# Transformer block with experts on Trainium2: low float16 parts of q, k and the attention output by VectorE from PSUM, in place of a ScalarE copy and a GpSimd subtraction

## Chip, cores and metric

One core of a Trainium2 chip (trn2). The metric is the device time of one execution in microseconds; lower is better.

## The reference, cut to what matters

Eight batches of 512 tokens of width 256 pass an adaptive layer norm, attention with 16 heads of 16, a second layer norm and a mixture of 2 shared and 16 routed experts (4 of 16 chosen for a token), all in float32:

```python
h = _layernorm(x, axis=-1) * (1 + ca) + sa
q, k, v = (split_heads(h @ w + b) for w, b in ((wq, bq), (wk, bk), (wv, bv)))
attn = softmax(einsum('bhqd,bhkd->bhqk', q, k) / 4)
o = einsum('bhqk,bhkd->bhqd', attn, v)            # heads merged
x = x + ga * (o @ wo + bo)
h = _layernorm(x, axis=-1) * (1 + cb) + sb
shared = gelu(h @ shared_up.T) @ shared_down.T     # 2 experts
routed = (gelu(h @ routed_up.T) * gate) @ routed_down.T  # 16 experts, gate from the top 4 probabilities
x = x + gb * (shared + routed)
```

## The kernel before, in words

**Split operands.** TensorE multiplies float16. A float32 value v is held as hi = float16(v) and lo = float16(v - hi), and a product is the sum of three: hi·hi, lo·hi and hi·lo (`split_product`). This concerns the layer norm's rows transposed (h1T, h2T: h and z), the attention output transposed (onT: z), q and k (qk), the experts' activations (act) and the weights.

**How a low part is made.** For h1T, h2T, onT and qk the result stands in a PSUM bank. ScalarE (`split_out`, line 668) copies it to float16 (line 671, `qk_hi`, `z_hi`, `h_hi`), then a second time as float32 into one of the two slots of `f_ring` in SBUF (line 673); this copy gives the bank back to TensorE (semaphore `taken[kind]`). GpSimd, which has no access to the bank in this kernel, then subtracts (`lo_part`, line 592): lo = f_ring - hi. The low part's own semaphore lets its users go on (the output projection for onT, the store to HBM for qk), and frees the slot of `f_ring`.

**Order.** All five engines walk one list, `PLAN`, written by a planner from tables of places, and each does the part of an item that is its own, in this order. A "slot" of the list is one group of 16 score products for the maxima (kind max: TensorE makes scores 128x512, VectorE takes their row maxima, line 907), one group of 16 for the softmax of an earlier group (kind exp: TensorE, then ScalarE, line 715), the value products (pv, line 1026; o_raw at line 898 is the copy of their result), and experts of an earlier batch: up (line 950, then gelu, line 750), gated (VectorE times the gate, line 894), act_hi (ScalarE, line 692), act_lo (GpSimd, line 651), down (line 1118). The maxima of four groups are transposed (maxT) and put by ScalarE or VectorE into the operand `q_aug`, from which the scores of kind exp then come with the maximum subtracted. Before item group 6 (about 180 us) there are no experts' products to fill the gaps; from there on the work repeats from batch to batch.

**Banks.** VectorE's items have three PSUM banks (`vector_bank`), ScalarE's three (`scalar_bank`), the experts' sums two (`down_bank`, lent to the others until the experts begin). Each item takes the bank that was used longest ago, and TensorE waits until that user's result has been taken (`wait_bank`). The order and the bank of every item are fixed when the program is built.

**The units that the change touches.** qk: 2 units for b = 0 (its first scores come from a shorter way, kind first) and 4 for each other batch, 30 in all, here called first to fourth unit of a batch; onT: 2 for each batch, 16 in all. Those of q and k of batch b stand in the slots that handle the scores of batch b - 1.

**GpSimd early on.** The item "fill" (lines 597 to 601) sets constants in the second pair of score operands and in `v_aug`; then come the steps of the layer norm's reciprocal deviation (line 584 to 586), for which VectorE's `rows` of the next batch (line 767) wait.

## Time and profile before

| | us |
|---|---|
| median of 3 runs | 887.67 |
| lowest, highest | 886.67, 888.42 |
| the profiled execution | 887.85 |
| its span, first to last instruction | 886.1 |
| TensorE busy (matmul) | 834.1, 94% |
| weight loads, beside them | 450.5, 51% |
| VectorE | 607.6, 69% |
| ScalarE | 681.8, 77% |
| GpSimd | 395.8, 45% |

In the profile PE is TensorE, PEld its weight loads, DVE VectorE, ACT ScalarE, POOL GpSimd. "L907" is line 907 of the kernel. A name such as `neg_max<-vector_bank` says what an instruction writes and reads, "128x512 f32" its shape and type, "x484" how many there are. In the timeline, neighbours of one form are merged to one row with their number; a bracket tells how long the engine was idle before, and what ended it. "Granted clock" is TensorE's clock as a share of 2.4 GHz; its mean over the span is 0.976, and in the stretches from 180 to 785 us it is 1.00.

### The profile page before, as it was taken

The page shows a single profiled execution, that of the slowest core. Times are in us where ns is not written, and L with a number is a line of the kernel's source. Part 1 is how long each engine was busy: PE and PEld are TensorE (multiplying, and loading weights), DVE is VectorE, ACT ScalarE, POOL GpSimd, SP SyncE. Part 2 cuts the span into 40 slices and gives each one's busy share as a digit, 9 for nine tenths or more (in the row PEclk, how much of TensorE's full clock was granted, in tenths as well). Part 3 has the DMA queues.
Part 4 walks back from the last instruction along what each step waited for, and adds up shares of the span by engine and source line. Part 5 has one row for each costly group of instructions (what it writes and reads, how often), then busy time and mean ns, then how long its engine had stood idle before and what let it go on. Part 6 is the DMA issues. An engine that isn't in the chain of part 4 may idle for free.

```text
span 886.1 us, 19423 instructions
## 1 busy us (share of the span) xinstructions
PE 834.1 (94%) x7652; PEld 450.5 (51%) x7652; DVE 607.6 (69%) x1211; ACT 681.8 (77%) x1158; POOL 395.8 (45%) x349
## 2 busy tenths in 40 slices
PE   5858788999999999999999999999999999998998
PEld 4322133355545575566545655566555554555555
DVE  4675677777688866977588776976687668632452
ACT  5468878878997789878988889878987788855452
POOL 4365215224744255335633464426623263346472
PEclk9987889899999999999999999999999999999999
DMA  7024400344025221424025402431314300330140
GB/s 259 13 75 131 137 13 14 97 127 138 13 61 175 90 61 52 148 62 138 25 68 169 138 2 73 154 100 25 105 48 149 119 2 1 133 120 1 61 163 26
DMA packets 47290, 77.18 MB, mean 87 GB/s; under 512 B 6392, under 2 KB 41432, under 8 KB 43104
## 3 DMA queue, kind: packets, MB, share of 16 engines
q1 hardware_dynamic: 47200, 75.94, 27.1%
q8 instruction: 61, 1.00, 0.5%
q14 instruction: 29, 0.24, 0.1%
HBM read 63.47 MB, written 12.34 MB: 86 GB/s over the span
## 4 chain that ended last, share of the span: by engine, by line
PE 74%; ACT 9%; DVE 8%; POOL 4%; issue 3%; DMA 0%; ACTq 0%; DVEq 0%
PE scalar_bank L950 21%; PE down_bank L1118 18%; PE vector_bank L1026 9%; PE scalar_bank L1009 6%; PE vector_bank L1009 6%; PE vector_bank L950 5%; DVE neg_max L907 3%; PE scalar_bank L1038 3%; ACT q_aug L701 2%; ACT probs L715 2%; PE vector_bank L1050 2%; ACT rows L684 1%; DVE gelu L894 1%; ACT f_ring L673 1%; PE scalar_bank L1062 1%
## 5 line engine op out<-in xcount | busy, mean ns | idle before, releaser
L907 DVE TENSOR_REDUCE neg_max<-vector_bank 128x1 f16<-128x512 f32 x484 | 306.7, 686 | 84.9 <-PE vector_bank L1009 75.6
L715 ACT ACTIVATE probs<-scalar_bank 128x512 f32<-128x512 f32 x486 | 262.3, 605 | 41.9 <-PE scalar_bank L1009 39.2
L651 POOL TENSOR_TENSOR act_lo<-gelu,act_hi 128x512 f16<-128x512 f32 x144 | 172.7, 1217 | 164.9 <-ACT act_hi L692 146.8
L1118 PE MATMUL down_bank<-down_hi,act_hi 64*128 64x256 f16 x1120 | 174.8, 271 | 0.4 <-PE down_bank L1118 0.2
L1118 PE MATMUL down_bank<-down_lo,act_hi 64*128 64x256 f16 x1120 | 173.7, 269 | 0.0
L1118 PE MATMUL down_bank<-down_hi,act_lo 64*128 64x256 f16 x1120 | 173.7, 269 | 0.0
L1009 PE MATMUL vector_bank<-k_aug,q_aug 64*128 64x512 f16 x484 | 132.9, 393 | 13.9 <-ACT q_aug L701 7.4
L894 DVE TENSOR_TENSOR gelu<-gelu,gates 128x512 f32<-128x512 f32 x128 | 110.3, 882 | 47.7 <-ACT gelu L750 47.4
L1009 PE MATMUL scalar_bank<-q_aug,k_aug 64*128 64x512 f16 x486 | 126.3, 389 | 3.9 <-ACT probs L715 1.7
L750 ACT ACTIVATE gelu<-scalar_bank 128x512 f32<-128x512 f32 x144 | 85.0, 596 | 57.6 <-PE scalar_bank L950 39.0
L1026 PE MATMUL vector_bank<-probs,v_aug 128*32 128x512 f32 x992 | 117.0, 601 | 0.0
L950 PE MATMUL scalar_bank<-z_hi,up_hi 128*128 128x512 f16 x288 | 109.9, 382 | 0.0
L950 PE MATMUL scalar_bank<-z_lo,up_hi 128*128 128x512 f16 x288 | 109.5, 380 | 0.0
L950 PE MATMUL scalar_bank<-z_hi,up_lo 128*128 128x512 f16 x288 | 109.4, 380 | 0.0
L692 ACT ACTIVATE act_hi<-gelu 128x512 f16<-128x512 f32 x128 | 76.8, 624 | 25.3 <-DVE gelu L894 19.0
L1118 PEld LDWEIGHTS down_bank<-down_hi,act_hi 64*128 64x128 f16 x1120 | 70.3, 94 | 47.8 <-issue 36.3
L1118 PEld LDWEIGHTS down_bank<-down_lo,act_hi 64*128 64x128 f16 x1120 | 74.8, 94 | 8.2
L1118 PEld LDWEIGHTS down_bank<-down_hi,act_lo 64*128 64x128 f16 x1120 | 74.7, 94 | 4.9
L1009 PEld LDWEIGHTS vector_bank<-k_aug,q_aug 64*128 64x128 f16 x484 | 37.1, 95 | 57.0 <-DVE neg_max L907 21.8
L592 POOL TENSOR_TENSOR z_lo<-f_ring,z_hi 128x512 f16<-128x512 f32 x32 | 36.6, 1155 | 56.5 <-ACT f_ring L673 56.5
L1009 PEld LDWEIGHTS scalar_bank<-q_aug,k_aug 64*128 64x128 f16 x486 | 37.3, 94 | 45.4 <-ACT probs L715 21.7
L1026 PEld LDWEIGHTS vector_bank<-probs,v_aug 128*32 128x32 f32 x992 | 27.5, 109 | 62.2 <-issue 56.6
(200 smaller groups left out, 1255.2 us busy)
## 6 DMA issues: line engine op xcount, KB each, us to landing
gates<-gates_by_expert SPq DMA_DIRECT2D x32, 1024.0 KB, 5.2
q_aug<-q_parts SPq DMA_DIRECT2D x90, 64.0 KB, 2.7
k_aug<-k_parts SPq DMA_DIRECT2D x90, 64.0 KB, 3.1
x_pre<-in_x SPq DMA_DIRECT2D x8, 512.0 KB, 4.6
x_post<-in_x SPq DMA_DIRECT2D x8, 512.0 KB, 6.5
out<-x_post SPq DMA_DIRECT2D x16, 256.0 KB, 3.6
gates<-in_w_up SPq DMA_DIRECT2D x4, 576.0 KB, 11.2
gates<-in_w_down SPq DMA_DIRECT2D x4, 576.0 KB, 4.5
```

The source lines that it names most:

```text
L592: pool.tensor_tensor(lo, f_ring[:, F_RING[kind, n, b][0], :], hi, ALU.subtract).then_inc(s_lo, 1)
L651: pool.tensor_tensor(act[1][:, c, :], gelu[:, n % NGELU, :], act[0][:, c, :], ALU.subtract).then_inc(s_elo, 1)
L692: scalar.activation(act[0][:, act_slot(b, n), :], gelu[:, n % NGELU, :], ACT.Copy).then_inc(s_ehi, 1)
L715: scalar.activation(probs[:, n % U, :], src[:], ACT.Exp, scale=SCALE).then_inc(taken[kind], 1)
L750: scalar.activation(gelu[:, n % NGELU, :], src[:], ACT.Gelu).then_inc(taken[kind], 1)
L894: dve.tensor_tensor(g, g, gates[:, (n - NSH) % 8, :], ALU.mult).then_inc(s_gated, 1)
L907: dve.tensor_reduce(neg_max[:, (u // 2) % TT, at:at + 1], src[:], AX.X, ALU.max, negate=True).then_inc(done, 1)
L950: ins = pe.matmul(dst, a, b, start=n == 0, stop=n == len(terms) - 1)
L1009: pe.matmul(dst[:], st[at:at + 64, pair, t * P:(t + 1) * P], mo[at:at + 64, pair, :], start=True, stop=True).then_inc(sig, 1)
L1026: ins = pe.matmul(o, v_aug[b % 2][:, kc, h * VW:h * VW + 32], probs[:, u, :], start=kc == 0, stop=kc == TT - 1)
L1038: ins = pe.transpose(dst[:, t * P:(t + 1) * P], a[:, t, n * P:(n + 1) * P], ident[:])
L1118: ins = pe.matmul(o, act[a][at:at + 64, act_slot(b, c), tok:tok + P], wd[w][at:at + 64, c, :], start=n == 0 and k == 0, stop=c == NEX - 1 ...
```

## The change

The units qk and onT no longer use `f_ring`. ScalarE makes the high part alone and signals it (`qk_hi_made`, `attention_hi_made`). VectorE, at the unit's own place in the list, waits for that signal and makes the low part in one instruction from the PSUM bank: for qk (bank + bias) - hi, for onT bank - hi. The semaphore of the low part is now also the one that gives the bank back to TensorE. GpSimd does nothing for these units. h1T, h2T and first are as before, and have the two slots of `f_ring` to themselves. TensorE's order is unchanged.

```diff
-F_KINDS = ("first", "onT", "h1T", "qk", "h2T")
+F_KINDS = ("first", "h1T", "h2T")
...
+        hi_made = {"qk": sem("qk_hi_made"), "onT": sem("attention_hi_made")}
+        taken["qk"], taken["onT"] = s_qklo, s_onlo
...
-                elif kind == "qk":
-                    lo_part(kind, n, b, qk[0][:, n % 2, :], qk[1][:, n % 2, :], s_qklo)
...
-                elif kind == "onT":
-                    lo_part(kind, n, b, z[0][:, n, :], z[1][:, n, :], s_onlo)
...
-                    split_out(item, src[:], qk[0][:, n % 2, :], ACT.Identity, bias=bqk[:, n % 2 * 2 + n // 2:n % 2 * 2 + n // 2 + 1])
+                    scalar.activation(qk[0][:, n % 2, :], src[:], ACT.Identity,
+                                      bias=bqk[:, n % 2 * 2 + n // 2:n % 2 * 2 + n // 2 + 1]).then_inc(hi_made["qk"], 1)
...
-                    split_out(item, src[:], z[0][:, n, :], ACT.Copy)
+                    scalar.activation(z[0][:, n, :], src[:], ACT.Copy).then_inc(hi_made["onT"], 1)
...
+                elif kind == "qk":
+                    wait(dve, hi_made["qk"], 4, b, n + 1 - SKIPPED["qk"])
+                    dve.scalar_tensor_tensor(qk[1][:, n % 2, :], bank(item)[:], bqk[:, n % 2 * 2 + n // 2:n % 2 * 2 + n // 2 + 1],
+                                             qk[0][:, n % 2, :], ALU.add, ALU.subtract).then_inc(s_qklo, 1)
+                elif kind == "onT":
+                    wait(dve, hi_made["onT"], 2, b, n + 1)
+                    z = z2[b % 2]
+                    dve.tensor_tensor(z[1][:, n, :], bank(item)[:], z[0][:, n, :], ALU.subtract).then_inc(s_onlo, 1)
```

VectorE around the second and third q and k unit of b = 3 (the timeline's 240 to 253 us; line 907 of before is line 914 of the change, 898 is 897, 939 is 946). Before:

```order
L894 TENSOR_TENSOR gelu<-gelu,gates 128x512 [waits taken_up] x3
L907 TENSOR_REDUCE neg_max<-vector_bank 128x1 [waits made_max] x2
L898 COPY o_raw<-vector_bank 128x512 [waits made_pv,made_oT]
L907 TENSOR_REDUCE neg_max<-vector_bank 128x1 [waits made_max] x12
L939 COPY logits<-vector_bank 128x64 [waits made_logit]
```

and with the change:

```order
L893 TENSOR_TENSOR gelu<-gelu,gates 128x512 [waits taken_up]
L900 SCALAR_TENSOR_TENSOR qk_lo<-scalar_bank,bqk,qk_hi 128x512 [waits qk_hi_made]
L893 TENSOR_TENSOR gelu<-gelu,gates 128x512 [waits taken_up] x2
L914 TENSOR_REDUCE neg_max<-vector_bank 128x1 [waits made_max] x2
L897 COPY o_raw<-vector_bank 128x512 [waits made_pv,made_oT]
L914 TENSOR_REDUCE neg_max<-vector_bank 128x1 [waits made_max] x2
L900 SCALAR_TENSOR_TENSOR qk_lo<-scalar_bank,bqk,qk_hi 128x512 [waits qk_hi_made]
L914 TENSOR_REDUCE neg_max<-vector_bank 128x1 [waits made_max] x4
L900 SCALAR_TENSOR_TENSOR qk_lo<-scalar_bank,bqk,qk_hi 128x512 [waits qk_hi_made]
L914 TENSOR_REDUCE neg_max<-vector_bank 128x1 [waits made_max] x6
L946 COPY logits<-vector_bank 128x64 [waits made_logit]
```

Three low parts now stand in the row, one between gate products and two between maxima.

VectorE around the fourth unit of b = 3 (260 to 267 us), where the router's last steps (865 to 873 of the change, 866 to 874 of before) stand. Before:

```order
L907 TENSOR_REDUCE neg_max<-vector_bank 128x1 [waits made_max] x2
L894 TENSOR_TENSOR gelu<-gelu,gates 128x512 [waits taken_up]
L866 TENSOR_REDUCE top<-e 128x4 [waits router_exp]
L894 TENSOR_TENSOR gelu<-gelu,gates 128x512 [waits taken_up]
L869 RECIPROCAL top<-top 128x4 [waits router_steps]
L871 TENSOR_TENSOR chosen<-chosen,e 128x64 [waits router_steps]
L874 TENSOR_TENSOR chosen<-chosen,top 128x64 [waits router_steps]
L898 COPY o_raw<-vector_bank 128x512 [waits made_pv,made_oT]
```

and with the change:

```order
L914 TENSOR_REDUCE neg_max<-vector_bank 128x1 [waits made_max] x2
L900 SCALAR_TENSOR_TENSOR qk_lo<-scalar_bank,bqk,qk_hi 128x512 [waits qk_hi_made]
L893 TENSOR_TENSOR gelu<-gelu,gates 128x512 [waits taken_up]
L865 TENSOR_REDUCE top<-e 128x4 [waits router_exp]
L893 TENSOR_TENSOR gelu<-gelu,gates 128x512 [waits taken_up]
L868 RECIPROCAL top<-top 128x4 [waits router_steps]
L870 TENSOR_TENSOR chosen<-chosen,e 128x64 [waits router_steps]
L873 TENSOR_TENSOR chosen<-chosen,top 128x64 [waits router_steps]
L897 COPY o_raw<-vector_bank 128x512 [waits made_pv,made_oT]
```

The low part comes ahead of both gate products and of the router's steps.

GpSimd around "fill" (43 to 55 us). Before:

```order
L629 TENSOR_TENSOR q_aug<-f_ring,act_hi 128x512 [waits taken_first]
L592 TENSOR_TENSOR qk_lo<-f_ring,qk_hi 128x512 [waits taken_qk]
L598 MEMSET q_aug 128x2048
L599 MEMSET k_aug 128x2048
L601 MEMSET v_aug 128x1152 x2
L584 TENSOR_SCALAR rstd<-mean_var 128x4 [waits ln1_steps]
```

and with the change:

```order
L631 TENSOR_TENSOR q_aug<-f_ring,act_hi 128x512 [waits taken_first]
L600 MEMSET q_aug 128x2048
L601 MEMSET k_aug 128x2048
L603 MEMSET v_aug 128x1152 x2
L586 TENSOR_SCALAR rstd<-mean_var 128x4 [waits ln1_steps]
```

The fills follow the operand of kind first directly.

## Rows read from the trace of the kernel before

**Rows 1.** the page's busy times; one stage: busy us by engine, clock, DMA
```profile
PE 834.1 (94%) x7652; PEld 450.5 (51%) x7652; DVE 607.6 (69%) x1211; ACT 681.8 (77%) x1158; POOL 395.8 (45%) x349
221.00:319.00 98.00, 97.73 (x959) 55.76 (x959) 75.50 (x151) 83.87 (x143) 45.22 (x40) 1.00 0.30 90
```

**Rows 2.** groups of instructions: busy us, mean ns of one, idle before them
```profile
L673 ACT ACTIVATE f_ring<-scalar_bank,bqk 128x512 f32<-128x512 f32 x28 | 19.3, 689 | 0.0
L592 POOL TENSOR_TENSOR qk_lo<-f_ring,qk_hi 128x512 f16<-128x512 f32 x30 | 35.5, 1184 | 42.4 <-ACT f_ring L673 42.4
L926 DVE TENSOR_TENSOR rows<-vector_bank,ga_all 128x512 f32<-128x512 f32 x15 | 10.4, 692 | 25.4 <-PE vector_bank L950 25.4
```

**Rows 3.** timeline, third unit, b = 3: start us, us, instruction, [idle before]
```profile
248.88 0.68 ACT L671 ACTIVATE qk_hi<-scalar_bank,bqk 128x512 f16<-128x512 f32 x1
249.16 3.08 DVE L907 TENSOR_REDUCE neg_max<-vector_bank 128x1 f16<-128x512 f32 x5 [0.91 <-PE vector_bank L1009]
249.83 0.47 PE L1009 MATMUL vector_bank<-k_aug,q_aug 64*128 64x512 f16 x2
```

**Rows 4.** timeline, attention output of b = 1
```profile
221.08 0.60 ACT L671 ACTIVATE z_hi<-scalar_bank 128x512 f16<-128x512 f32 x1
221.58 0.59 ACT L673 ACTIVATE f_ring<-scalar_bank 128x512 f32<-128x512 f32 x1
222.49 2.49 DVE L907 TENSOR_REDUCE neg_max<-vector_bank 128x1 f16<-128x512 f32 x4 [0.69 <-PE vector_bank L1009]
223.17 0.47 PE L1009 MATMUL vector_bank<-k_aug,q_aug 64*128 64x512 f16 x2
```

**Rows 5.** timeline, fourth unit of b = 3
```profile
262.19 0.69 ACT L671 ACTIVATE qk_hi<-scalar_bank,bqk 128x512 f16<-128x512 f32 x1
261.99 1.19 DVE L894 TENSOR_TENSOR gelu<-gelu,gates 128x512 f32<-128x512 f32 x1
263.93 1.09 DVE L871 TENSOR_TENSOR chosen<-chosen,e 128x64 f32<-128x64 f32 x1
265.05 1.08 DVE L874 TENSOR_TENSOR chosen<-chosen,top 128x64 f32<-128x64 f32 x1
266.05 0.68 DVE L898 COPY o_raw<-vector_bank 128x512 f32<-128x512 f32 x1
263.53 1.40 POOL L592 TENSOR_TENSOR qk_lo<-f_ring,qk_hi 128x512 f16<-128x512 f32 x1 [0.90 <-ACT f_ring L673]
264.90 2.27 POOL L651 TENSOR_TENSOR act_lo<-gelu,act_hi 128x512 f16<-128x512 f32 x2
266.45 0.72 PE L1009 MATMUL vector_bank<-k_aug,q_aug 64*128 64x512 f16 x2
```

**Rows 6.** timeline, fourth unit of b = 0 and what follows
```profile
46.88 1.15 POOL L592 TENSOR_TENSOR qk_lo<-f_ring,qk_hi 128x512 f16<-128x512 f32 x1 [2.55 <-ACT f_ring L673]
43.74 1.29 DVE L907 TENSOR_REDUCE neg_max<-vector_bank 128x1 f16<-128x512 f32 x2 [2.18 <-PE vector_bank L1009]
54.96 4.18 DVE L767 TENSOR_SCALAR rows<-x_pre,mean_var,rstd 128x256 f32<-128x256 f32 x4 [0.58 <-POOL rstd L586]
59.28 1.09 PE L1038 MATMUL down_bank<-ident,rows 128*128 128x128 f32 x4 [6.04 <-DVE rows L767]
```

**Rows 7.** timeline, third unit of b = 1
```profile
87.38 2.17 DVE L907 TENSOR_REDUCE neg_max<-vector_bank 128x1 f16<-128x512 f32 x3 [0.43 <-PE vector_bank L1009]
88.71 0.69 ACT L671 ACTIVATE qk_hi<-down_bank,bqk 128x512 f16<-128x512 f32 x1
```

**Rows 8.** the chain that ended last: start us, us, what
```profile
138.50 3.68 DVE neg_max L907 x6
```

**Rows 9.** busy time and clock of two stretches, columns as above
```profile
157.40:160.70 3.30, 2.99 (x10) 0.84 (x8) 1.29 (x2) 2.78 (x6) 1.97 (x3) 0.50 0.24 79
727.00:731.00 4.00, 2.56 (x36) 1.75 (x31) 1.90 (x4) 3.97 (x7) 1.15 (x1) 1.00 0.00 0
```

**Rows 10.** timeline, a router product of b = 0, GpSimd idle
```profile
167.06 0.20 DVE L871 TENSOR_TENSOR chosen<-chosen,e 128x64 f32<-128x64 f32 x1
```

## The prediction, made before the changed kernel ran

> **What bounds the kernel now.** I read the page's first part, then the busy time by stage, then the granted clock, then the timeline of each place that the change touches. TensorE is busy 94% of the span, and in the repeating part of the kernel (one batch every 97.3 us from 221 us on, by the starts of like instructions) it is busy 97.7 of 98 us at full clock, with VectorE at 75.5, ScalarE at 83.9 and GpSimd at 45.2 [rows 1]. So from about 180 us on an engine that is relieved gives nothing by itself: TensorE has no waits to give back. But TensorE works strictly in its written order, and three banks of VectorE and three of ScalarE are all it can run ahead by. What VectorE does late there, TensorE waits for, and no later gap takes it back. Before 180 us it is otherwise: TensorE has gaps, one of 6.04 us at 53 to 59 us [rows 6].
>
> **What is removed.** 46 second copies by ScalarE (30 of q and k, 16 of the attention output; b = 0 has only two q and k units, the others four) of about 0.69 us [rows 2]; the next instruction starts 0.5 to 0.6 after such a copy began, since they overlap [rows 4]; and 46 subtractions by GpSimd of 1.18 us [rows 2], 54 us of its 396. After 180 us I cost both at nothing, since TensorE's own work covers them.
>
> **What is added.** 46 VectorE instructions with one operand in PSUM and one in SBUF. None of this form with float16 output is in the trace; the nearest, the product of the output projection with its gate (same size, same sources), takes 0.69 us [rows 2]. Five maxima in a row take 3.08 us [rows 3], so an instruction that follows another costs 0.60. I take 0.60 behind another and 0.69 to its end; bounds 0.60 and 1.19 (a product of this size from SBUF alone, beside GpSimd's work [rows 5]). What matters more is the wait: the new instruction stands in VectorE's order at the unit's own place and waits for ScalarE's high part. All maxima behind it wait too, though their banks are full. TensorE waits for these maxima's banks, and the transposes of a row group's maxima wait for all of them. The bank of the unit itself is given back by VectorE too: some 0.2 us later than by ScalarE's second copy; its next user comes later than that in nearly all places.
>
> **The places.** For each I took the end of ScalarE's high part, the end of VectorE's instruction before it, and the start of the one behind it. In the repeating part there are five:
>
> 1. Third q and k unit of a batch. The high part runs 248.88 to 249.56, VectorE's next maxima start at 249.16 [rows 3]. They now start at 249.6 + 0.6 = 250.23: 1.07 late. TensorE's pair of score products at 249.83 takes 0.47 instead of 0.38 because the second already waits for the first of these maxima; it comes 1.07 late. Five batches: **+5.3** (bounds 2.5 and 6.5).
> 2. The two units of the attention output. The first high part runs 221.08 to 221.68, the second copy begins 0.50 behind it, the next maxima at 222.49 [rows 4]. With the second high part in that copy's place, ending near 222.2, the two low parts run from 221.73 and 222.33, the maxima from 222.94: 0.45 late, and again a TensorE pair (223.17, 0.47 long) waits for the first of them. Six batches: **+2.7** (0 and 5.4).
> 3. Fourth q and k unit. The high part ends at 262.88, VectorE's next instruction, a gate product, started at 261.99 [rows 5] and now starts at 263.5. Behind it on VectorE stand the last steps of the router, then the copy of o_raw (266.05), for whose bank TensorE waits in its pair at 266.45, 0.72 long [rows 5]. Some of the 1.5 comes back: the two router products took 1.09 and 1.08 beside GpSimd's work, the same took 0.20 beside an idle GpSimd [rows 5, 10]. The Trainium skill ("SBUF — State Buffer", who interferes with whom) calls the pair of ports that VectorE and GpSimd share an exclusive lock, taken by a VectorE instruction with two SBUF inputs against a GpSimd one that reads; the trace agrees, the first of them ends 0.09 us after GpSimd's subtraction. The removed subtraction frees the first product, but ScalarE's act_hi waits for the late gate product, so act_lo (two, 2.27 us together [rows 5]) now starts near 265.1 and ends near 267.4, over both router products. I take o_raw 1.3 late, four times, and 0.6 the fifth time, where the unit stands one step later: **+5.8** (0 and 8).
> 4. First and second units: the first costs a gate product 0.6, which ScalarE, busy with other work, does not feel; the second 0.15, with 0.5 to spare on TensorE's side. **0** (0 and 2).
>
> Before 180 us:
>
> 5. b = 0, fourth unit. GpSimd's subtraction at 46.88 waits 2.55 us for ScalarE's copy and ends at 48.03; behind it on GpSimd stand the fills and rstd, for which VectorE's rows wait (54.96, 4.18 long), then TensorE at 59.28 after 6.04 idle [rows 6]. Without it the fills can begin 2.55 + 1.15 = 3.7 us sooner. But VectorE's maxima at 43.74 wait until 46.9, which brings TensorE 2.1 late and the statistics and values with it. I take **-2.0** (-3.7 and 0).
> 6. b = 1, third unit. The high part ends at 89.40; three maxima from 87.38 [rows 7] start at 90.1 instead, and three further products wait in turn: **+1.7** (0.9 and 2.2).
> 7. b = 0, attention output: it stands in a row of six maxima, 3.68 us on the chain that ended last [rows 8]; two more at 0.6: **+1.2** (0 and 1.5).
> 8. The other q and k units there, looked at the same way, give +0.5, -0.2, -0.5, +0.2 and +0.5: **+0.5** (-1 and 3).
>
> TensorE is busy 2.56 of 4.00 us from 727 on, where it waits for ScalarE [rows 9]; that takes back the last 0.5 of place 2: **-0.5**. For b = 7 nothing is taken.
>
> Sum: 5.3 + 2.7 + 5.8 + 0 - 2.0 + 1.7 + 1.2 + 0.5 - 0.5 = **+14.7 us**. The profiled execution took 887.85 (span 886.1 and 1.75 around it), 0.02% over the median 887.67, so no correction: 887.9 + 14.7 = **902.6 us**, 1.7% slower. A measurement of this kernel can tell about 0.2%, 1.8 us, from no change.
>
> **The rivals.**
>
> *GpSimd's lock gives place 3 back.* Alone, the two router products take 0.4 together instead of 2.17, and the gate product 0.7 instead of 1.19 [rows 5, 10]. If act_lo comes behind them, the gain of 2.3 is more than the push of 1.5, and o_raw is on time: 902.6 - 5.8 = 896.8. By the skill's rule in place 3 the order in which they are issued decides; by the rule this would be 896.8 and by my reading of the order 902.6. For it: GpSimd is idle from 262.6 on. Against: act_hi needs only the first gate product, and act_lo follows at once. Chance 0.17.
>
> *Relief wins, the other side.* VectorE idles 22 us per batch, ScalarE 14. If the maxima that are pushed back had their banks asked for later than I read (the wait at the pairs 249.83 and 223.17 being mere issue), places 1 to 3 cost nothing, and place 5 and the 0.5 us per copy in the early part decide: 887.9 - 2.0 to -3.7 = 884 to 886. It decides as soon as the bank of the first pushed maximum is wanted over 1.1 us after its old release; in rows 3 it is wanted 0.1 us after it. Chance 0.05.
>
> *The clock falls.* The trace has the granted clock at 0.50 from 157.4 to 160.7, behind TensorE waits of 1.6 us, in a stage with many gaps [rows 9]. A stretch of that length at half clock costs 1.7 us. If each of the nine waits of over 1 us in the repeating part brings one, it is +15 more: 918. Against: in the 1.44 us that TensorE lacks from 727 to 731 [rows 9] the clock stayed at 1.00. Chance 0.06.
>
> *It does less than it says.* If ScalarE were so far behind that the units waited anyway, or VectorE took the low parts in its idle time, the change would be near 0, 886 to 890. Chance 0.03. The rest, 0.69, is the forecast with its bounds.
>
> **How the numbers follow.** The forecast's bounds, not all met at one end, are 895 to 909; the lock case reaches to 893. The range 893 to 909 leaves out the clock, the relief and the null cases and some of the forecast's ends. Faster by over 0.2%: the relief case less a part that lies within, 0.05. Within: 0.04. Slower: 0.91.
>
> **What would show it.** Right: in the repeating part a batch takes about 99.9 us instead of 97.3; TensorE waits for neg_max and o_raw in it of 0.5, 1.1 and 1.3 us; VectorE waits for ScalarE's qk_hi and z_hi; the rows of place 5 earlier; TensorE's gap at 53 us shorter. Place 3 is wrong if the router products take 0.2 to 0.3 us and o_raw keeps its place behind TensorE's products. The whole is wrong if batches still take 97.3 us, or if the clock in the repeating part is below 1.00.

## The result, and the profile after

| | us |
|---|---|
| before, median of 4 runs | 887.17 |
| changed kernel, median of 4 runs | 906.29 |
| lowest, highest | 905.87, 908.17 |
| ratio, 95% interval | 1.0212 (1.0197 to 1.0227) |
| the profiled execution, its span | 908.17, 906.3 |

The change makes the kernel 2.1% slower, 18.6 us over the median of the table ahead of the prediction. The profiled execution is the slowest of its four; the others took 905.9 to 906.3. That difference fits a phase of the clock, told below. One timed run of the kernel before, beside experiments 9 to 11, took 906.5 us at a mean granted clock of 0.931, against 886.2 to 890.8 for all others timed beside the experiments; the ratios leave it out.

The page of the changed kernel, busy times and granted clock in 40 slices; then one window of 100 us in the repeating part, columns as in [rows 1]:

```profile
PE 846.2 (93%) x7652; PEld 453.3 (50%) x7652; DVE 632.7 (70%) x1257; ACT 661.0 (73%) x1112; POOL 343.1 (38%) x303
PEclk9777879999999999999999999999999999999999
```

```profile
229.00:329.00 100.00, 98.74 (x964) 56.25 (x964) 78.31 (x157) 81.52 (x138) 38.19 (x35) 1.00 0.30 89
```

Compared with [rows 1], ScalarE has 21 us less to do and GpSimd 53, as the change says. VectorE has 25 us more (46 instructions more). None of the relief is on the path: TensorE still does the same 7652 products, at full clock in the window, and now waits in it. For b = 4 to 6 a batch takes 100.26 us instead of 97.4 (start of one score product to that of the same one a batch later), near the 99.9 that the prediction named as its sign.

Groups of the changed kernel (busy us, mean ns of one, idle before them), the new instructions first, and what the answer for `qk_lo` says of VectorE's idle time before them:

```profile
L900 DVE SCALAR_TENSOR_TENSOR qk_lo<-scalar_bank,bqk,qk_hi 128x512 f16<-128x512 f32 x28 | 21.0, 748 | 32.1 <-ACT qk_hi L732 32.1
L905 DVE TENSOR_TENSOR z_lo<-scalar_bank,z_hi 128x512 f16<-128x512 f32 x15 | 9.7, 685 | 1.4 <-ACT z_hi L737 1.4
L1016 PE MATMUL vector_bank<-k_aug,q_aug 64*128 64x512 f16 x484 | 138.0, 392 | 25.2 <-DVE neg_max L914 12.5 <-ACT q_aug L699 6.5 <-DVE o_raw L897 5.5
  ACT qk_hi L732: 34.8, 23
```

A new instruction takes 0.69 to 0.75 us, but VectorE stands still for 34.8 us in 23 waits for ScalarE's high part. Much of this takes the place of other waits: its idle time before the maxima fell from 84.9 to 61.5 us. What matters is what is queued behind each wait. TensorE's products for the maxima wait 12.5 us for VectorE's maxima and 5.5 for its copy of o_raw. In the kernel before, the same group waited 4.4 and 1.6.

To see where time is lost, take the start of each of TensorE's 1024 score products in both profiles, in order, and subtract. This difference, here called the **lag**, stays constant where nothing is lost and steps where a product comes late:

| place (start in before) | lag before it | step, b by b |
|---|---|---|
| up to 34.9 us, ahead of every changed unit | 0 | +2.4 (clock) |
| 34.9 to 62 us | 2.4 | +6.8 by 53 us, all given back by 62 |
| 77 to 93 us, third unit of b = 1 | 2.8 | +2.9 |
| 93 to 181 us | 5.7 | +2.5 |
| attention output, b = 1 to 6 | 8.15 | +0.42, 0.46 x5 |
| third unit, b = 3 to 7 | | +0.97 to 0.99, five times |
| fourth unit, b = 3 to 7 | | +0.19, +1.41, +1.41, +1.41, +0.33 |
| end | 20.5 | 0 |

Early part 8.15, repeating part 12.4.

Third unit of b = 3 in the timeline of the changed kernel, to be held beside [rows 3]:

```profile
257.35 0.68 ACT L732 ACTIVATE qk_hi<-scalar_bank,bqk 128x512 f16<-128x512 f32 x1
258.06 0.75 DVE L900 SCALAR_TENSOR_TENSOR qk_lo<-scalar_bank,bqk,qk_hi 128x512 f16<-128x512 f32 x1 [1.35 <-ACT qk_hi L732]
258.73 3.71 DVE L914 TENSOR_REDUCE neg_max<-vector_bank 128x1 f16<-128x512 f32 x6
259.47 0.39 PE L1016 MATMUL vector_bank<-k_aug,q_aug 64*128 64x512 f16 x1 [0.80 <-DVE neg_max L914]
```

The maxima start at 258.73. On the old order they would have at 249.16 + 8.57 (the lag at this point) = 257.73: 1.0 late, and TensorE follows.

Attention output of b = 1, to be held beside [rows 4]:

```profile
229.24 1.09 ACT L737 ACTIVATE z_hi<-scalar_bank 128x512 f16<-128x512 f32 x2
229.88 1.28 DVE L905 TENSOR_TENSOR z_lo<-scalar_bank,z_hi 128x512 f16<-128x512 f32 x2
231.07 2.48 DVE L914 TENSOR_REDUCE neg_max<-vector_bank 128x1 f16<-128x512 f32 x4
```

Without the change the four maxima would start at 222.49 + 8.15 = 230.64; they are 0.43 late.

Fourth unit of b = 3 and of b = 4. The first four rows (b = 3) show a place where 0.19 is lost, the rest (b = 4) one where 1.41 is:

```profile
274.55 0.20 DVE L870 TENSOR_TENSOR chosen<-chosen,e 128x64 f32<-128x64 f32 x1
...
274.62 2.27 POOL L649 TENSOR_TENSOR act_lo<-gelu,act_hi 128x512 f16<-128x512 f32 x2 [2.43 <-ACT act_hi L690]
...
274.78 1.08 DVE L873 TENSOR_TENSOR chosen<-chosen,top 128x64 f32<-128x64 f32 x1
...
275.78 0.68 DVE L897 COPY o_raw<-vector_bank 128x512 f32<-128x512 f32 x1
...
371.61 0.75 DVE L900 SCALAR_TENSOR_TENSOR qk_lo<-scalar_bank,bqk,qk_hi 128x512 f16<-128x512 f32 x1 [0.83 <-ACT qk_hi L732]
...
373.76 2.27 POOL L649 TENSOR_TENSOR act_lo<-gelu,act_hi 128x512 f16<-128x512 f32 x2 [2.43 <-ACT act_hi L690]
...
374.32 0.68 DVE L870 TENSOR_TENSOR chosen<-chosen,e 128x64 f32<-128x64 f32 x1
...
375.04 1.08 DVE L873 TENSOR_TENSOR chosen<-chosen,top 128x64 f32<-128x64 f32 x1
...
376.04 0.68 DVE L897 COPY o_raw<-vector_bank 128x512 f32<-128x512 f32 x1
...
376.78 0.39 PE L1016 MATMUL vector_bank<-k_aug,q_aug 64*128 64x512 f16 x1 [1.25 <-DVE o_raw L897]
```

For b = 3 the first router product starts at 274.55, just ahead of act_lo at 274.62, and takes 0.20. Only the second is held, and o_raw, at 275.78, is 0.2 late (266.05 [rows 5] and the lag of 9.54 give 275.59). From b = 4 on one more router step (line 862, 0.59 us) lies between the gate products and this one, so both products start behind act_lo, and end at 375.00 and 376.12, with the two halves of act_lo. So the rival "GpSimd's lock gives place 3 back" happened in one batch of five, and there for one of the two products.

**The clock, ahead of every changed unit.** Two windows of the profiled executions, columns as above, the changed kernel's first, then the kernel before's:

```profile
27.00:37.00 10.00, 9.64 (x32) 4.88 (x30) 4.51 (x9) 1.44 (x2) 1.15 (x1) 0.50 0.01 2
```

```profile
27.00:31.00 4.00, 3.43 (x24) 2.04 (x21) 3.59 (x7) 1.45 (x2) 1.15 (x1) 1.00 0.02 4
31.30:34.30 3.00, 3.00 (x10) 1.24 (x10) 0.93 (x3) 0.00 (x0) 0.00 (x0) 0.50 0.01 3
```

The granted clock fell to its lower level (1.2 GHz) at 26.8 us for 10 us in the one, at 31.0 for 3 us in the other, where both still run the same instructions. This is the +2.4. The profiles of experiments 1, 2 and 6 have it too (lag 2.2 to 2.4 by 35 us), in those of 5 and 7 the clock fell twice for 3 us, in that of 4 at 30.6 for 7 us, and in all profiles but those of the change and of 1, 2 and 6 the lag by 35 us is -0.1 to 0.3. It goes with the execution rather than with the kernel: experiments 6, 8 and 10 run the same instructions in the same order up to 233 us, and the clock fell at 26.9 us for 10 us in the profile of 6, at 32.1 and 31.5 for 3 us in those of 8 and 10. The three faster runs of the changed kernel have a mean clock of 0.974 and 0.975, the profiled one 0.970.

### The profile page after: what moved, and what is told of

It is laid out like the page before. It is cut to its first block, busy times and chain, and to the rows that moved or that the text cites. A ratio compares the mean times of both kernels' runs of the same rounds, so it can differ in the third digit from the quotient of the medians.

```text
span 906.3 us, 19377 instructions
## 1 busy us (share of the span) xinstructions
PE 846.2 (93%) x7652; PEld 453.3 (50%) x7652; DVE 632.7 (70%) x1257; ACT 661.0 (73%) x1112; POOL 343.1 (38%) x303
## 4 chain that ended last, share of the span: by engine, by line
PE 73%; DVE 14%; ACT 8%; issue 3%; POOL 2%; DMA 0%; ACTq 0%; DVEq 0%
PE scalar_bank L957 23%; PE down_bank L1125 16%; PE vector_bank L1033 10%; DVE neg_max L914 7%; PE scalar_bank L1016 6%; PE vector_bank L1016 5%; PE vector_bank L957 5%; ACT probs L713 2%; ACT f_ring L671 1%; ACT q_aug L699 1%; DVE qk_lo L900 1%; PE scalar_bank L1069 1%; PE scalar_bank L1045 1%; PE vector_bank L1057 1%; ACT qk_hi L732 1%
## 5 line engine op out<-in xcount | busy, mean ns | idle before, releaser
L914 DVE TENSOR_REDUCE neg_max<-vector_bank 128x1 f16<-128x512 f32 x484 | 306.3, 685 | 61.5 <-PE vector_bank L1016 54.0
L1125 PE MATMUL down_bank<-down_hi,act_lo 64*128 64x256 f16 x1120 | 175.6, 269 | 0.0
L1125 PE MATMUL down_bank<-down_lo,act_hi 64*128 64x256 f16 x1120 | 175.6, 269 | 0.0
L1016 PE MATMUL vector_bank<-k_aug,q_aug 64*128 64x512 f16 x484 | 138.0, 392 | 25.2 <-DVE neg_max L914 12.5
L1016 PE MATMUL scalar_bank<-q_aug,k_aug 64*128 64x512 f16 x486 | 129.4, 391 | 5.2 <-ACT probs L713 1.7
L690 ACT ACTIVATE act_hi<-gelu 128x512 f16<-128x512 f32 x128 | 77.0, 625 | 34.8 <-DVE gelu L893 27.9
L1125 PEld LDWEIGHTS down_bank<-down_hi,act_hi 64*128 64x128 f16 x1120 | 70.8, 94 | 47.4 <-issue 34.3
L699 ACT ACTIVATE q_aug<-vector_bank 1x512 f16<-1x512 f16 x68 | 40.0, 588 | 13.5 <-PE vector_bank L1022 12.9
```

What stands on the lines that cost most here:

```text
L690: scalar.activation(act[0][:, act_slot(b, n), :], gelu[:, n % NGELU, :], ACT.Copy).then_inc(s_ehi, 1)
L699: ins = scalar.activation(q_aug[b % 2][at:at + 1, 2 * n + j // 2, :], bank(item)[:].bitcast(F16)[32 * j:32 * j + 1, 0:S], ACT.Copy)
L914: dve.tensor_reduce(neg_max[:, (u // 2) % TT, at:at + 1], src[:], AX.X, ALU.max, negate=True).then_inc(done, 1)
L1016: pe.matmul(dst[:], st[at:at + 64, pair, t * P:(t + 1) * P], mo[at:at + 64, pair, :], start=True, stop=True).then_inc(sig, 1)
L1125: ins = pe.matmul(o, act[a][at:at + 64, act_slot(b, c), tok:tok + P], wd[w][at:at + 64, c, :], start=n == 0 and k == 0, stop=c == NEX - 1 ...
```

## The experiments

All kernels of this section can make a unit's low part in either way. `by_vector(item)` names the units that VectorE takes; the others go the old way (second copy by ScalarE, subtraction by GpSimd, two semaphores instead of one). `DEFER` holds a low part back behind so many of VectorE's following items. With all units and an empty `DEFER` the order is that of the changed kernel, with none that of the kernel before. The lag is always against the profile of before shown ahead. The kernel before, timed beside them, took 888.24 (experiments 1 to 4), 888.57 (5 to 8) and 888.99 (9 to 11); the ratios are against the runs beside them. They are estimated from all runs and are not quite the quotients of the medians (for experiment 2 these give 1.0060).

| | run | median us | ratio, 95% interval | lag at 194 us | at 721 us |
|---|---|---|---|---|---|
| | the change | 906.29 | 1.0212 (1.0197 to 1.0227) | 8.2 | 20.5 |
| 1 | early units the old way | 903.12 | 1.0162 (1.0134 to 1.0189) | 2.4 | 14.7 |
| 2 | attention output alone | 893.60 | 1.0041 (1.0022 to 1.0060) | 3.7 | 6.2 |
| 3 | third unit one maximum later | 902.09 | 1.0156 (1.0133 to 1.0179) | 8.2 | 16.7 |
| 4 | fourth unit two products later | 904.75 | 1.0202 (1.0164 to 1.0240) | 6.5 | 16.8 |
| 5 | q and k of b = 0 alone | 888.36 | 1.0005 (0.9994 to 1.0016) | -1.8 | -1.9 |
| 6 | the same, four maxima later | 886.09 | 0.9978 (0.9968 to 0.9989) | -0.7 | -0.7 |
| 7 | all, moved | 897.45 | 1.0105 (1.0091 to 1.0120) | 0.4 | 6.9 |
| 8 | the free places | 888.64 | 0.9994 (0.9981 to 1.0007) | -1.5 | -0.2 |
| 9 | q and k of b = 1, 2 alone | 891.90 | 1.0042 (1.0028 to 1.0057) | 4.1 | 4.0 |
| 10 | as 8, without b = 7 | 886.85 | 0.9982 (0.9971 to 0.9992) | -2.9 | -2.0 |
| 11 | as 7, fourth one step later | 897.89 | 1.0113 (1.0093 to 1.0133) | -0.5 | 7.4 |

### 1. The early units the old way

```diff
+def by_vector(item):
+    kind, n, b = item
+    return kind == "qk" and b > 2 or kind == "onT" and b > 0
```

> Units that are handled before 180 us (q and k of b = 0 to 2, attention output of b = 0) are made the old way, the others as in the change. Theory (the loss is made at the places, one by one; TensorE's score products of the change lag those of before by 8.2 us at 190 us and by 20.5 us at 730 us): the time is before + 12.3 us, 899.5 us, and the lag grows by 0.47, 0.97 and 1.41 us a batch as before. Rival (the early part's loss is a matter of the granted clock, which fell 4 us earlier before any changed unit had run, and comes in any kernel with an altered GpSimd or VectorE order): some of the 8 us stays, 903 us or more.

Measured: 903.12, ratio 1.0162. By the time alone this is the rival's number, 3.6 us over the theory's. The lag tells what it is made of: it is +2.2 by 35 us, the same early fall of the clock as in the profile of the change. Then it stays at 2.3 to 2.4 until 222 us, and then it makes the steps of the change again, one for one (0.41, 0.98, 0.19, 0.46, 0.99, 1.41, 0.46 and so on), to 14.7. So the rival holds for the 2.2 that come ahead of every changed unit, and not for the rest. The early and the repeating part are separate costs: the units before 180 us cost 8.15 - 2.36 = 5.8, those behind 12.4, with two steps (1.0 and 0.6) near 770 us on top, where the clock was 0.50 from 767.5 to 770.6.

### 2. The attention output alone

```diff
+    return kind == "onT"
```

> Only the attention output's low parts by VectorE, q and k the old way. Theory: six places at 0.47 us, less 0.5 taken back, and about 1.2 us at the one of b = 0: +3 to +4 us, 890.5 us. Rival (the waits of one unit are what makes those of the others cost): less than 1 us, 888 us.

Measured: 893.60, ratio 1.0041, which is 3.6 us. The nine runs lie in two groups, four of 890.2 to 891.7 us at a mean clock of 0.978 and five of 893.6 to 894.0 at 0.972 to 0.974; the profiled one is of the second. Beside the clock's +2.2, the unit of b = 0 costs 1.5 net (lag 2.24 at 35 us, 3.73 at 185), each of the six next 0.36 to 0.44, together 2.5: 4.0. None is given back at the end (the lag is 6.2 at 716 and at 779 us in the old times), and the unit of b = 7 costs nothing.

### 3. The third unit one maximum later

```diff
+    return kind in ("qk", "onT")
+DEFER = {("qk", 2, b): 1 for b in range(3, 8)}
```

> As the change, but the low part of the third q and k unit of b = 3 to 7 stands one maximum later in VectorE's order. The work on VectorE is the same; only the wait for ScalarE lies behind a maximum. Theory (the wait at the head of VectorE's order, not the added work, is the cost): the step of 0.97 us a batch becomes 0.2 to 0.3, 5 x 0.7 = 3.6 us less than the change, 902.7 us. Rival (added VectorE work is the cost): no change, 906.3 us.

Measured: 902.09, ratio 1.0156, 4.2 us under the change. The timeline at the place of b = 3:

```profile
257.37 0.69 ACT L781 ACTIVATE qk_hi<-scalar_bank,bqk 128x512 f16<-128x512 f32 x1
257.64 0.69 DVE L973 TENSOR_REDUCE neg_max<-vector_bank 128x1 f16<-128x512 f32 x1 [0.91 <-PE vector_bank L1075]
258.25 0.74 DVE L874 SCALAR_TENSOR_TENSOR qk_lo<-scalar_bank,bqk,qk_hi 128x512 f16<-128x512 f32 x1
...
258.91 3.07 DVE L973 TENSOR_REDUCE neg_max<-vector_bank 128x1 f16<-128x512 f32 x5
```

The maximum fills the time until the high part is there, and the low part then waits for nothing. It still takes VectorE 0.66 us, but the step of 0.97 in the lag has become one of 0.22, in each of the five batches; the fourth unit's steps are those of the change. So of the third unit's cost the larger part was the wait with the maxima queued behind it, and the smaller the added work. In the profiled execution, the slowest of four, the clock fell for 3 us at 769 us.

### 4. The fourth unit two gate products later

```diff
+DEFER = {("qk", 3, b): 2 for b in range(3, 8)}
```

> As the change, but the low part of the fourth q and k unit of b = 3 to 7 stands behind the next two gate products in VectorE's order. Its bank is asked for 3.9 us later than it is released before. Theory: the gate products and ScalarE's act_hi come on time, o_raw 0 to 0.3 us late instead of 1.4: 4 us less than the change, 902.3 us. Rival (the lock between GpSimd's act_lo and the router's products decides, whatever the place): o_raw stays over 1 us late, 906 us.

Measured: 904.75, ratio 1.0202, with one run of 909.51 among four; the times alone settle little here, the lag does. The step of the fourth unit is 0.6 instead of 1.41 for b = 4 to 6 (0.2 again for b = 3, and 0.7 instead of 0.33 for b = 7); the other steps are those of the change. So the repeating part costs 2.0 us less, half of the 4 expected, and o_raw comes neither on time nor over 1 us late. At b = 4:

```profile
370.78 0.74 DVE L874 SCALAR_TENSOR_TENSOR qk_lo<-scalar_bank,bqk,qk_hi 128x512 f16<-128x512 f32 x1
371.05 2.29 POOL L696 TENSOR_TENSOR act_lo<-gelu,act_hi 128x512 f16<-128x512 f32 x2 [1.35 <-ACT act_hi L737]
...
372.28 1.14 DVE L937 TENSOR_TENSOR chosen<-chosen,e 128x64 f32<-128x64 f32 x1
...
373.45 0.23 DVE L940 TENSOR_TENSOR chosen<-chosen,top 128x64 f32<-128x64 f32 x1
...
373.60 0.68 DVE L964 COPY o_raw<-vector_bank 128x512 f32<-128x512 f32 x1
...
374.34 0.39 PE L1075 MATMUL vector_bank<-k_aug,q_aug 64*128 64x512 f16 x1 [0.45 <-DVE o_raw L964]
```

Now the gate products come on time. With the lags taken off (9.5 here, 11.2 in the change) act_lo starts 1.1 us sooner than in the change, and it ends as the first router product does: the second takes 0.23. The copy of o_raw follows the end of act_lo (373.34 here, 376.03 in the change) in both.

### 5. The q and k units of b = 0 alone

```diff
+    return kind == "qk" and b == 0
```

> VectorE makes the low parts of the two q and k units of b = 0 alone; all others go the old way. Theory: GpSimd's fills start 3.7 us or more sooner, but VectorE's maxima, which wait for ScalarE's high part, come about 2 us late, TensorE and the statistics with them, and the gap at 53 to 59 us only gives back what was lost: shift of TensorE's score products at 62 us within 0.5 us of the old, total within 0.5 us of before (886.7 to 888.3). Rival, the step on record: 2.0 us faster, 885.2 to 886.2. Second rival: the early part of the whole change (8 us late at 189 us) comes from b = 0, then 3 us or more slower, over 890.5.

Measured: 888.36 against 888.57, ratio 1.0005: no difference. The profiled execution was the fastest of twelve (886.03) and has a lag of -1.8. Its timeline:

```profile
47.09 0.75 DVE L874 SCALAR_TENSOR_TENSOR qk_lo<-scalar_bank,bqk,qk_hi 128x512 f16<-128x512 f32 x1 [4.70 <-ACT qk_hi L781]
...
56.11 0.75 DVE L1000 TENSOR_TENSOR v_aug<-vector_bank,bv_all 128x256 f32<-128x256 f32 x2 [3.05 <-PE vector_bank L1016]
56.79 2.04 DVE L819 TENSOR_SCALAR rows<-x_pre,mean_var,rstd 128x256 f32<-128x256 f32 x4
...
45.09 1.81 POOL L643 MEMSET q_aug<- 128x2048 uint32 x1
...
52.22 1.04 POOL L628 TENSOR_TENSOR rstd<-rstd,minus_half 128x4 f32<-128x4 f32 x1
```

GpSimd's fills start at 45.09 instead of 47.97, and its rstd at 52.22 instead of 53.81. But VectorE's rows start at 56.79, not sooner than the 54.96 of [rows 6], and end at 58.83, 0.3 sooner than the 59.14 there. Ahead of them in VectorE's order stands the sum for `v_aug`, which before waited for GpSimd's fill and now waits 3.05 us for TensorE. TensorE is late because four maxima stood behind VectorE's wait of 4.70 us, and because the clock was low from 49.7 to 56.5. How much is owed to each, no run takes apart; in all four profiles with the low part at this place (the change, 3, 4 and 5) the clock fell at 47.6 to 50.7 us, and in the five with it moved (6, 7, 8, 10 and 11) the clock was full from 47.4 to 56. The chain has another last member: the relief of GpSimd is real, and all but 0.3 us of it unused. Most of the lag of -1.8 is the clock's: the transposes behind the rows start 0.3 us sooner (58.97 for 59.28), and by 62 us the lag is -1.4, in a stretch where the clock was full here (56.5 to 66.7) and low in the kernel before (58.3 to 75.4).

### 6. The same, four maxima later

```diff
+DEFER = {("qk", 3, 0): 4}
```

> As the run before, but VectorE makes the low part of the fourth unit of b = 0 four maxima later, so no maximum waits for ScalarE's high part. Theory: the relief of GpSimd is kept and nothing is paid: VectorE's rows start 2 to 3.7 us sooner, TensorE's gap at 53 us is 2 to 3.7 us shorter, and the time 884 to 886. Rival: something else holds the rows back (ScalarE's or VectorE's statistics), then within 0.5 us of before.

Measured: 886.09, ratio 0.9978, 2.3 us under experiment 5 and, by the ratio, 2.0 under before, at the upper edge of what was expected. TensorE's gap at this place:

```profile
59.20 0.63 PE L1104 MATMUL down_bank<-ident,rows 128*128 128x128 f32 x4 [2.34 <-DVE rows L819]
```

It is 2.34 us instead of 6.04 [rows 6], in part because TensorE comes to it later: in this profile the clock fell early (+2.4 by 35 us). With these 2.4 taken off, the transposes of the rows start at 56.8 instead of 59.28, 2.5 us sooner. With no maximum behind the wait the relief comes through. From 35 us to the end the kernel gained 3.1 in this profile, and 2.0 by the times; the stretches at the lower clock lie otherwise than in the kernel before, so the difference may be theirs.

### 7. All 46 units, moved

```diff
+DEFER = {("qk", 3, 0): 4, ("qk", 0, 1): 1, ("qk", 2, 1): 3, **{("qk", 2, b): 1 for b in range(3, 8)}, **{("qk", 3, b): 2 for b in range(3, 8)}}
```

> The whole change, all 46 low parts by VectorE, with those places moved where maxima or router steps waited: the fourth unit of b = 0 four maxima later, the first and third of b = 1 by one and three, the third of b = 2 to 7 by one, the fourth of b = 3 to 7 by two steps. Theory: the 0.97 steps vanish, the fourth unit costs 0.6 three times, the attention output still 0.45 seven times, the early part about 2 us: 893 to 896. Rival: the cost is VectorE's added work or its slower release of the banks, wherever it stands: 902 or more.

Measured: 897.45, 1.5 us above the range expected and well under the rival's. Half of the change's cost is gone with the same work on every engine. In the lag the early part costs 0.4 (2 were expected), the attention output as before, the fourth unit 0.2 for b = 3, 0.6 for b = 4 to 6 and 0.7 for b = 7. What the expectation lacked is 0.2 at each third unit, and 1.6 at 760 us, where the clock fell for 3 us.

### 8. Only the places that cost nothing

```diff
+    return kind == "qk" and (b == 0 or b > 2 and n < 3)
```

(with the `DEFER` of experiment 7)

> By VectorE only what costs nothing by the theory: the two units of b = 0 (fourth four maxima later) and the first three units of b = 3 to 7 (third one maximum later); the rest the old way. 17 low parts of 46. Theory: no step in TensorE's lag after 180 us, the gain of the run with b = 0 alone kept: 884 to 887. Rival: VectorE's load in the repeating part costs by itself: 889 or more.

Measured: 888.64, ratio 0.9994: the expectation was too low by 1.6 us and more, and the time is next to the rival's. The lag of the profiled execution (889.43) shows why: -3.1 at 62 us and -1.5 at 185, with the clock's stretches lying otherwise between them (in the profile of experiment 10, the same instructions up to 233 us, the lag goes from -3.3 only to -2.9 there), then 0.25 lost in each of five batches (at the third unit: one more instruction of 0.66 in a row of six maxima is not quite free), and 1.6 at 753 us, where the clock fell. TensorE waits 1.57 us for o_raw up to 751.26; the window behind it:

```profile
752.30:755.30 3.00, 3.00 (x23) 1.43 (x20) 1.82 (x4) 1.09 (x2) 0.00 (x0) 0.50 0.00 0
```

### 9. The q and k units of b = 1 and 2 alone

```diff
+    return kind == "qk" and b in (1, 2)
```

> VectorE makes the low parts of the eight q and k units of b = 1 and 2 alone, at the change's own places. Theory: these eight carry what the early part of the whole change lost over the forecast: 4 us, the time 892 to 894; TensorE's lag at 185 us 3.5 to 4.5. Rival, the terms on record (+1.7 and +0.5): 890.5 to 891. Second rival: the early loss came from the clock and not from waits, then within 1 us of before (888.6).

Measured: 891.90, ratio 1.0042, which is 3.7 us; the lag at 194 us is 4.1. This fits the first reading better than the terms on record, and shows how the third unit of b = 1 costs more than its wait:

```profile
89.14 0.75 DVE L874 SCALAR_TENSOR_TENSOR qk_lo<-down_bank,bqk,qk_hi 128x512 f16<-128x512 f32 x1 [2.28 <-ACT qk_hi L781]
89.80 1.88 DVE L973 TENSOR_REDUCE neg_max<-vector_bank 128x1 f16<-128x512 f32 x3
89.94 0.39 PE L1075 MATMUL down_bank<-q_aug,k_aug 64*128 64x512 f16 x1 [0.98 <-DVE qk_lo L874]
```

```profile
90.50:97.00 6.50, 6.46 (x24) 1.11 (x28) 4.94 (x9) 2.84 (x7) 0.00 (x0) 0.50 0.34 103
```

VectorE stands for 2.28 us with three maxima behind it, and TensorE waits 0.98 for the low part itself, since the unit lies in one of the two lent banks, and that bank is wanted at once. The lag grows by 1.9 in the products up to 90.5 us (old times) and by 1.6 more in those up to 94.3, which fall into the window above, at the lower clock. In the kernel before the clock was 1.00 there and 0.50 from 103 to 109, and there 1.1 comes back. The other 1.6 come between 120 and 185 us, at the units of b = 2, in stretches where the clock differs too.

### 10. As 8, without the last batch

```diff
+    return kind == "qk" and (b == 0 or 2 < b < 7 and n < 3)
```

> As the mixed version (17 low parts by VectorE), but without the three units of b = 7: 14 low parts. Theory: the mixed version lost its gain where the clock fell at 752 us behind waits in b = 7 (1.5 us) and by 0.27 in each of five batches; here no fall at 752 and four times 0.27: 886.5 to 887.5. Rival: the fall at 752 comes whatever b = 7 does, or the loss is elsewhere: 888.3 or more.

Measured: 886.85, ratio 0.9982, as expected in time, but not for the reason given. The same wait is there, and the clock did not fall behind it:

```profile
749.52 0.39 PE L1075 MATMUL vector_bank<-k_aug,q_aug 64*128 64x512 f16 x1 [1.58 <-DVE o_raw L964]
```

```profile
751.00:755.00 4.00, 4.00 (x57) 2.82 (x52) 3.40 (x7) 3.39 (x8) 0.00 (x0) 1.00 0.10 27
```

The kernel before waits 1.57 there too, at full clock behind it. In the profiles of experiments 1, 3, 7 and 8 the clock fell behind this place for 3 us, in all others it did not. Which of the two comes is not settled by this wait, nor by whether b = 7 is changed. What else decides it stays open. So it also stays open how much of experiment 8's miss is owed to its three units of b = 7.

### 11. The fourth unit behind o_raw

```diff
-... **{("qk", 3, b): 2 for b in range(3, 8)}}
+... **{("qk", 3, b): 3 for b in range(3, 8)}}
```

> As the run with all 46 low parts moved, but the fourth unit of b = 3 to 7 one step later still, behind the copy of o_raw, so that neither the router's last products nor o_raw stand behind it. Theory: o_raw on time, only the four maxima behind it 0.6 late: the step of 0.82 in TensorE's lag becomes 0.3 to 0.6, total 1 to 2 us under 897.45: 895.5 to 896.5. Rival: the router's products are held by act_lo whatever stands ahead of them, or the later release of the bank costs the same: 897 or more.

Measured: 897.89, ratio 1.0113, no better than experiment 7 and what the rival had. First experiment 7 at b = 4, then this one:

```profile
363.14 0.74 DVE L874 SCALAR_TENSOR_TENSOR qk_lo<-scalar_bank,bqk,qk_hi 128x512 f16<-128x512 f32 x1
363.41 2.28 POOL L696 TENSOR_TENSOR act_lo<-gelu,act_hi 128x512 f16<-128x512 f32 x2 [1.35 <-ACT act_hi L737]
...
365.95 0.68 DVE L964 COPY o_raw<-vector_bank 128x512 f32<-128x512 f32 x1
366.55 2.47 DVE L973 TENSOR_REDUCE neg_max<-vector_bank 128x1 f16<-128x512 f32 x4
```

```profile
362.10 2.28 POOL L696 TENSOR_TENSOR act_lo<-gelu,act_hi 128x512 f16<-128x512 f32 x2 [1.35 <-ACT act_hi L737]
...
364.38 0.68 DVE L964 COPY o_raw<-vector_bank 128x512 f32<-128x512 f32 x1
...
364.99 0.73 DVE L874 SCALAR_TENSOR_TENSOR qk_lo<-scalar_bank,bqk,qk_hi 128x512 f16<-128x512 f32 x1
365.64 2.47 DVE L973 TENSOR_REDUCE neg_max<-vector_bank 128x1 f16<-128x512 f32 x4
366.38 0.39 PE L1075 MATMUL vector_bank<-k_aug,q_aug 64*128 64x512 f16 x1 [0.87 <-DVE neg_max L973]
```

o_raw starts 2.28 us behind act_lo's start instead of 2.54, as the theory has it, but the maxima start 3.54 behind it instead of 3.14, and the fourth unit's step in the lag is 1.0 instead of 0.6 for b = 4 to 6, and 1.3 instead of 0.7 for b = 7. Ahead of the router's products most of the low part's time is hidden, since the products end with act_lo anyway. Behind them it is paid in full. For b = 3, where the first product escapes act_lo, it is the other way: 0.23 is gained instead of 0.22 lost.

The kernel before, profiled once more:

> The kernel before, unchanged, profiled once more. Theory: the fall of the granted clock at 26 to 31 us, before any changed unit has run, comes at 31 in some executions and near 26.7 in others, and moves TensorE by about 2.2 us by 35 us; the medians of before (886.4 to 888.3, and 889.2 to 890.8) are these two. Either phase may show here. Rival: the phase goes with the kernel; then this one again falls at 31.2.

Measured: 888.11, and the clock as in the first profile:

```profile
31.30:34.30 3.00, 3.00 (x10) 1.24 (x10) 0.99 (x3) 0.00 (x0) 0.00 (x0) 0.50 0.01 3
```

The unchanged kernel was not caught in the early phase. Of its timed runs beside experiments 9 to 11 four have a mean clock of 0.970 to 0.972 and took 889.6 to 890.7 us, twelve 0.974 to 0.977 and 886.7 to 889.7; this fits phases some 2 us apart, but no profile of it shows one.

## Why the prediction was right, and where its sum was off

The forecast was 902.6 with a range of 893 to 909; measured were 906.3. The sum was +14.7. The profiled execution shows 12.4 in the repeating part, 5.8 in the early one and 2.4 of clock; the median shows 18.6, about the first two alone. By its steps:

1. **Third unit**, +5.3: five steps of 0.97 to 0.99, +4.9. Right in place, cause and size. Experiment 3 shows the cause: with the wait filled, all but 0.22 of each goes.
2. **Attention output**, +2.7 and 0.5 given back at 727 us: six steps of 0.42 to 0.46, +2.7. The size of one was right (0.45). The last one is not given back: TensorE's idle time there [rows 9] takes nothing back (lag 20.5 at 721 and at 779 us). Experiment 2 shows the same at an undisturbed place.
3. **Fourth unit**, +5.8: 0.19, 1.41, 1.41, 1.41, 0.33, +4.8. The mechanism was right: the low part waits, the gate products and with them act_lo come late, and VectorE's router products end with act_lo. TensorE's wait of 1.25 for o_raw, where rows 5 had the pair at 266.45, is the 1.3 of the text. For b = 3 the rival decided, in part by luck: the first product started 0.07 us ahead of act_lo. The Trainium skill's rule ("SBUF — State Buffer", who interferes with whom) calls the ports that VectorE and GpSimd share an exclusive lock. The traces agree: a product of 128x64 took 0.20 to 0.23 ahead of or behind act_lo and 0.68 to 1.14 while it ran, ending within 0.1 us of the end of one of its halves.
4. **First and second units**, 0: no lasting step at them in any profile. Right.
5. **b = 0, fourth unit**, -2.0: measured +0.4 by the ratio of experiment 5, its interval from -0.5 to +1.4; in the change the lag at 62 us is that at 35 us. This is the first step that failed. The text named both effects, GpSimd 3.7 us sooner and TensorE 2.1 late "and the statistics and values with it", and let the first win. The rows in VectorE's order stand behind the sum for v_aug, and that waits for TensorE's values, so the lateness decides the start of the rows. Experiment 6 shows that the relief was there to be had, 2.0 us, as soon as no maximum waits. The text also left out the clock, which was low at this place in every profile with the low part in it.
6. and 8. **q and k of b = 1 and 2**, +1.7 and +0.5: measured 3.7 by the ratio of experiment 9, 4.1 by its lag. This is the term that was mis-sized most. It priced the wait, and the wait was as read (for the three maxima from 87.38 [rows 7] it gave 90.1, and they start at 89.80). But it also said that the unit's own bank is wanted later than its new release "in nearly all places", and this one, in a lent bank, is not such a place; and in experiment 9 the wait is followed by a stretch at the lower clock (0.50 from 90.2 to 97.1 us), where the sum has the full one.
7. **b = 0, attention output**, +1.2: +1.5 in experiment 2. Right.

Taken together, 1.4 was given for the early part and 5.8 came, which the single experiments (0.4, 3.7 and 1.5) nearly add up to. The repeating part was given 13.3 and 12.4 came. The time lies in the range because the bounds of the early places, added up, reach from -3.8 to 6.7; the sum itself was 3.9 us short in a forecast of 14.7.

Of the rivals, the clock did not fall in the repeating part (1.00 in the window above), so +15 did not come. It did fall in other stretches of the early part than before, and in some kernels once near the end (1.6). Relief wins: in the change as it is, nowhere. In experiments 6 and 10 it did, at b = 0, once the low part stood where nothing waits behind it.

**A version that beats both.** Experiment 6, two of the 46 units by VectorE: 886.09, ratio 0.9978 (0.9968 to 0.9989), and experiment 10 with 14 units: 886.85, 0.9982 (0.9971 to 0.9992). Both gain at one place, TensorE's gap at 53 to 59 us; experiment 10 pays 0.25 for each of its four later batches. Experiment 8, with the same move at b = 0, was not faster (0.9994), so the gain of some 2 us is no larger than what else moves here. At none of the other places did a profile show a gain, save 0.23 once in experiment 11.

## What to carry to other kernels

- An instruction that is moved to an in-order engine costs less by its own time than by the wait it brings: here 0.6 to 0.7 us of work cost 0.22 behind one maximum, and 0.97 when that maximum stood behind the wait. Before moving work to an engine, look at what is queued behind it at that place, and whether a later place is as good for its users.
- Relief of an engine counts only if it ends the chain. Follow the chain's next member through the written order of every engine on it; here the fill came 2.9 us sooner and the last of the rows 0.3.
- Where VectorE must wait for the end of a long GpSimd instruction anyway, work put ahead of that end is the cheaper: the low part cost 0.6 us ahead of it and 1.0 behind it, for b = 4 to 6 (experiments 7 and 11).

## What the runs showed of the hardware that was not expected

- The granted clock fell at about 26.8 us for 10 us in four profiles, and at about 31 for 3 us in most others, of kernels that run the same instructions up to there; this moves TensorE by 2.2 to 2.4 us. A difference of 2 us between two single profiles of this kernel says nothing.
- Near the end a fall of 3 us (1.6 us lost) comes in 4 of 14 profiles; the wait of 1.57 us ahead of it is in profiles without the fall too.
- A VectorE instruction from PSUM and SBUF to float16 SBUF of 128x512 takes 0.685 us as a plain difference and 0.748 with a scalar per partition added; the low part of q and k was thus 0.06 dearer than the row it was estimated from [rows 2].
- Four `rows` (128x256, SBUF alone) took 4.18 us in the kernel before [rows 6], and 2.04 in experiment 5. The second of them, from 56.04 to 58.49, took 2.45 us beside one GpSimd instruction (`up_lo`, 55.93 to 58.34), and the two behind it 0.40 each with GpSimd idle. In experiment 6 it is the same (55.96 to 58.41, `up_lo` to 58.26), and in experiment 5 the first took 1.07 and ended at 57.85, `up_lo` at 57.71. So a row that meets a GpSimd instruction ends 0.14 to 0.15 us behind it. These have one tensor from SBUF and not two as the router products above; no run shows whether it is the same lock.
